# Two attention layers, a mixture layer and 64 experts on one core: a new order of pieces on every engine, and maxima rows in two transfers in place of four

## The chip, the cores and the metric

The kernel runs on one core of a Trainium2 chip. A core has a matrix engine (TensorE; PE in the profile, its weight loads PEld), a vector engine (VectorE, DVE), a scalar engine (ScalarE, ACT), GpSimd (POOL) and SyncE (SP), each with an instruction stream of its own. The streams meet only through semaphores. Transfers are issued by SP and POOL and carried out by 16 DMA engines. The metric is device time in microseconds (us) of one launch.

## The reference

The input x has 32 sequences of 256 tokens with 256 features; a context of the same shape belongs to it. Everything is float32. Cut to what matters:

```python
x = x + xattn0(layernorm(x), ctx, ctx, Wq, bq, Wk, bk, Wv, bv, Wo, bo)   # 16 heads of 16, softmax(q k^T / 4) v
x = x + mixture(layernorm(x), P_w, U1, U2, U3, W1, W2, b2)
x = x + xattn1(layernorm(x), ctx, ctx)                                  # 16 heads of 16, no projections
x = x + moe(layernorm(x), router_w, w_gate, w_up, w_down, ws_gate_up, ws_down)

# mixture: z_i = (x P_w^T) U_i^T; C_i = softmax over the 3 largest of 12
#   h = gelu(sum_e C1[:, e] * (x W1[e]^T));  y = sum_e C2[:, e] * (h W2[e]^T) + C3 b2
# moe: probs = softmax(x router_w^T), the 8 largest of 64, weights made to sum to 1;
#   each expert takes up to 128 tokens: y = (silu(g) * u) w_down;  plus a shared expert for every token
```

## The kernel before, in words

One batch is one sequence (128 tokens x 2 tiles). The 32 batches go through the four layers one behind the other, but overlapped: while PE works on the mixture of one batch, the attention of the layers around it stands between. After them 64 expert steps follow (loads of gathered rows, gate and up, down), which the change does not touch.

The work is cut into pieces, and each engine has one long string, `ORDERS[engine]`, in which each letter is one piece; the next piece of that kind is taken each time the letter comes (`pieces`). Nothing else sets the order of the work: each engine runs its string from front to back, and where a piece needs another engine it waits for that engine's semaphore, with all that stands behind it on its own engine waiting too. In the middle of the kernel (batches 5 to 29) each string repeats itself exactly from batch to batch.

A batch has two attention jobs (layer 0 and layer 1), a job has two halves of 8 heads, and a half u is made of these pieces:

- N, `spread`: SP copies the split keys and queries of the half from HBM into `kst` and `qst` (4 transfers of 192 KB, lines 529 and 532).
- O, `s1` (4 per half, L1286): PE forms the scores of two heads in the bank `first`. The next O may only write there when DVE has read the maxima off it (`nm`, L978).
- P, `max_rows`: DVE splits the maxima into a high and a low part (`nmp`, L988 and L990), PE turns them (L1294), ACT copies them (`mT`, L787), and SP puts them into `qst` as two further rows per pair of heads, by four transfers of one row (L540).
- Q, `s2` (4 per half, L1304): PE forms the scores again, less the maximum, in the bank `second`; ACT takes the exponent (`exps`, L793) before the next Q may write there.
- R, `av` (2 per half, L1320): PE multiplies with the values; ACT copies the result (`out_sb`, L800). S, `out_turn`, turns it back (L1331).

M, `mix` (24 per batch, L1386) is one expert of the mixture: 12 matmuls of 128x256 in three splits, in the two-part bank `mixp`; DVE adds the result with its weight (L1070), and M number n waits until DVE has done number n-2. Other letters that count here: F `d_turn` and v `h_turn` (turns of activations, L1212), J `d_up` (the shared expert's down product, L1443, which also writes to `first`), p `r_turn` (turn of the mixture's input; ACT copies it as `r_part_h`, L721, DVE forms the rest `r_part_l`, L888), q `r_z` (the routing scores, L1365, which read both). O and Q use 48 and 50 of the array's rows at a time, two heads beside each other; all else named here uses its full height.

The first batches and the last ones have orders of their own, since the pipeline fills and drains there. POOL scatters the rows of each batch to the experts' slots (L678, 16 per batch); its string holds the letters O too, and a scatter waits until PE has done the O that stands ahead of it there. The last 48 scatters stand behind the last O of half 127, one behind the other, and the expert steps load their rows behind the last of them.

Of the kernel before, what the change touches and what calls it, by code (L numbers as in the profile page):

```python
# [34 lines left out]
class Steps:  # L35
# [5 lines left out]
    def up(self):  # L41
# [16 lines left out]
        "LbPczNPNAgPajNPNLbPczNPNAgPajNPNLbPczNPNAgPajNPNLbPczNPNAgPjNPNLPzNPNAPPLzNNPALPzNANWWWPWWWWPWWWWWWWWWLL"
# [1521 lines left out]
```

## Time and profile before

| | before |
|---|---|
| median of 3 runs | 2767.86 us (2764.5 to 2769.37) |
| profiled execution | 2765.2 us, span 2763.4 us |
| PE busy | 2616.3 us, 95% of the span |
| PE weight loads (beside PE) | 2189.8 us, 79% |
| DVE busy | 2207.7 us, 80% |
| ACT busy | 1067.6 us, 39% |
| POOL busy | 811.1 us, 29% |
| mean granted TensorE clock | 0.984 of full |
| chain that ended last | PE 77%, DVE 12%, issue 4%, DMA 2% |

The span runs from the first to the last instruction; the 1.8 us that the execution takes beyond it lie around it. "Idle before" names the instruction that released the engine. Busy shares of PE and DVE are of pipelined instructions: two of them that overlap are counted from start to end together.

### The profile page before, as it was taken

To read this page: it belongs to the slowest core of one execution; us is meant where nothing else is said; L and a number is where in the kernel's file an instruction comes from. 1 tells how busy PE (TensorE), PEld (TensorE's weight loads), DVE (VectorE), ACT (ScalarE), POOL (GpSimd) and SP (SyncE) were. 2 spreads that over 40 slices of the span, in tenths; PEclk is the share of its full clock that TensorE was granted. 3 is DMA by queue.
4 is the path that set the end of the run, shared out by engine and by line. 5 is a ranking of instruction groups with operands and counts; after the bars stand their busy time and mean duration, and the time that the engine had idled before them with its cause. 6 is when DMAs were issued, how large, how long until landed. Compare 5 with 4: busy or idle time off the path is not lost.

```text
span 2763.4 us, 59981 instructions
## 1 busy us (share of the span) xinstructions
PE 2616.3 (95%) x22949; PEld 2189.8 (79%) x22949; DVE 2207.7 (80%) x6135; ACT 1067.6 (39%) x1622; POOL 811.1 (29%) x829
## 2 busy tenths in 40 slices
PE   3899999999999999999999999999999999985999
PEld 3778788888888888888888888888888888863776
DVE  5677888888888888888888888888888888762554
ACT  3333434444444444433444444444444344322332
POOL 1000133322323232322332232323232232226444
PEclk9999999999999999999999999999999999986999
DMA  7644444444444444443444444444344333245997
GB/s 226 174 141 107 114 127 129 124 109 115 118 118 110 117 112 97 117 118 93 107 112 99 107 117 112 109 112 113 89 106 109 93 98 83 55 87 157 230 234 169
DMA packets 322210, 336.02 MB, mean 122 GB/s; under 512 B 46676, under 2 KB 302751, under 8 KB 321412
## 3 DMA queue, kind: packets, MB, share of 16 engines
q1 hardware_dynamic: 286404, 307.37, 42.8%
q0 software_dynamic: 33792, 18.52, 4.0%
q10 hardware_dynamic: 1728, 6.29, 0.7%
q8 instruction: 182, 2.98, 0.5%
q14 instruction: 104, 0.85, 0.1%
HBM read 191.65 MB, written 221.81 MB: 150 GB/s over the span
## 4 chain that ended last, share of the span: by engine, by line
PE 77%; DVE 12%; issue 4%; DMA 2%; ACT 2%; POOL 2%; SPq 1%; POOLq 0%; ACTq 0%; DVEq 0%
PE mixp L1386 35%; PE attn_out L1320 6%; PE second L1304 5%; DVE nm L978 4%; PE first L1286 4%; DVE hid L1070 3%; PE misc L1254 3%; PE misc L1212 3%; PE mixp L1488 3%; PE misc L1422 2%; PE misc L1331 2%; PE second L1507 2%; PE misc L1461 2%; PE misc L1350 2%; PE first L1443 2%
## 5 line engine op out<-in xcount | busy, mean ns | idle before, releaser
L793 ACT ACTIVATE exps<-second 128x1024 f32<-128x1024 f32 x512 | 525.4, 1026 | 770.9 <-PE second L1304 763.6
L678 POOL DMA_INDIRECT expert_slots<-row_mem,sidx x512 | 510.4, 997 | 820.1 <-PE first L1286 579.1
L1386 PE MATMUL mixp<-w_h,r_part_h 128*128 128x256 f32 x3072 | 664.2, 297 | 2.3 <-DVE r_part_l L888 1.1
L978 DVE TENSOR_REDUCE nm<-first 128x4 f32<-128x1024 f32 x504 | 614.3, 1219 | 24.8 <-PE first L1286 24.2
L1386 PE MATMUL mixp<-w_h,r_part_l 128*128 128x256 f32 x3072 | 609.8, 280 | 0.0
L1386 PE MATMUL mixp<-w_l,r_part_h 128*128 128x256 f32 x3072 | 609.3, 279 | 0.0
L1386 PEld LDWEIGHTS mixp<-w_h,r_part_h 128*128 128x128 f32 x3072 | 467.8, 189 | 43.4 <-issue 2.1
L1386 PEld LDWEIGHTS mixp<-w_l,r_part_h 128*128 128x128 f32 x3072 | 468.8, 188 | 0.0
L1386 PEld LDWEIGHTS mixp<-w_h,r_part_l 128*128 128x128 f32 x3072 | 468.6, 188 | 0.0
L1070 DVE SCALAR_TENSOR_TENSOR x_mem<-mixp,C,x_mem 128x256 f32<-128x256 f32 x768 | 332.6, 477 | 74.5 <-PE mixp L1386 67.5
L1070 DVE SCALAR_TENSOR_TENSOR hid<-mixp,C,hid 128x256 f32<-128x256 f32 x704 | 303.6, 477 | 54.4 <-PE mixp L1386 52.9
L652 POOL TENSOR_TENSOR norm<-norm,minus_half 128x2 f32<-128x2 f32 x128 | 91.8, 717 | 694.9 <-DVE norm L917 694.9
L1320 PE MATMUL attn_out<-exps,vx 128*17 128x256 f32 x4096 | 273.8, 389 | 4.5 <-ACT exps L793 4.5
L1304 PE MATMUL second<-qst,kst 50*128 50x256 f32 x2048 | 254.5, 319 | 9.9 <-ACT exps L793 5.5
L1286 PE MATMUL first<-kst,qst 48*128 48x256 f32 x2016 | 232.1, 307 | 18.8 <-DMA qst<-q_parts 11.4
L1304 PEld LDWEIGHTS second<-qst,kst 50*128 50x128 f32 x2048 | 163.6, 189 | 84.1 <-issue 39.7
L1286 PEld LDWEIGHTS first<-kst,qst 48*128 48x128 f32 x2016 | 155.9, 188 | 53.1 <-DMA qst<-q_parts 11.7
L1320 PEld LDWEIGHTS attn_out<-exps,vx 128*17 128x17 f32 x4096 | 95.2, 98 | 101.0 <-issue 20.5
L689 POOL DMA_INDIRECT out<-x_mem,sidx x64 | 99.0, 1546 | 112.9 <-DVE sidx L1168 48.8
L725 ACT ACTIVATE nat_h<-misc,qk_cols 128x256 fp32r<-128x256 f32 x128 | 53.6, 470 | 152.3 <-PE misc L1254 147.5
L893 DVE SCALAR_TENSOR_TENSOR nat_l<-misc,qk_cols,nat_h 128x256 fp32r<-128x256 f32 x128 | 56.0, 479 | 61.1 <-ACT nat_h L725 61.1
L800 ACT COPY out_sb<-attn_out 128x512 f32<-128x512 f32 x128 | 74.5, 582 | 78.1 <-PE attn_out L1320 74.6
(236 smaller groups left out, 3593.1 us busy)
## 6 DMA issues: line engine op xcount, KB each, us to landing
kst<-k_parts SPq DMA_DIRECT2D x256, 192.0 KB, 4.1
qst<-q_parts SPq DMA_DIRECT2D x256, 192.0 KB, 4.5
q_parts<-nat_h SPq DMA_DIRECT2D x128, 256.0 KB
k_parts<-ctx_part_h SPq DMA_DIRECT2D x64, 256.0 KB, 2.5
k_parts<-nat_h SPq DMA_DIRECT2D x64, 256.0 KB, 5.6
q_parts<-nat_l SPq DMA_DIRECT2D x64, 256.0 KB
exps<-in_wgu SPq DMA_DIRECT2D x30, 384.0 KB, 4.2
expert_slots<-row_mem SPq DMA_DIRECT2D x16, 642.0 KB, 6.5
```

Source lines behind the costliest of these rows:

```text
L652: pool.e.tensor_tensor(rstd[kind][:, :], veps[kind][:, :], minus_half[:, :], ALU.pow).then_inc(p_pow[kind], 1)
L678: pool.e.indirect_dma_start(out=slots_dram, out_offset=bass.IndirectOffsetOnAxis(ap=sidx[b % 2][:, t, k:k + 1], axis=0), in_=row[b % 2][:, ...
L689: pool.e.indirect_dma_start(out=out_pad, out_offset=bass.IndirectOffsetOnAxis(ap=eid[e % NID], axis=0), in_=ey[e % NY], in_offset=None, bo ...
L793: act.e.activation(exps[:, j % NU, :, :, :].rearrange("p k t s -> p (k t s)"), second[:, :, :].rearrange("p k s -> p (k s)"), ACT.Exp, sca ...
L978: dve.e.tensor_reduce(nm[u % 2][:, :, 2 * j:2 * j + 2].rearrange("p t k -> p k t"), (mixp_mem if in_mixp(b, kind, j) else first)[:, :, :]. ...
L1070: dve.e.scalar_tensor_tensor(acc, src, c, acc, ALU.mult, ALU.add).then_inc(v_mix, 1)
L1212: m = pe.e.transpose(v[:, dt, t * P:(t + 1) * P], src[:, t, dt * P:(dt + 1) * P], ident)
L1254: m = pe.e.matmul(out, w[j][:, dt, c * P:(c + 1) * P], x[i][:, dt, :], start=(n == 0), stop=(n == 3 * DT - 1))
L1286: m = pe.e.matmul(bank[k][:, t * S:(t + 1) * S], q_st[u % 3][at, j, t * P:(t + 1) * P], k_st[u % 3][at, j, :], start=True, stop=True)
L1304: m = pe.e.matmul(bank2[k][:, s * S:(s + 1) * S], k_st[u % 3][at, j, s * P:(s + 1) * P], q_st[u % 3][at, j, :], start=True, stop=True)
L1320: m = pe.e.matmul(attn_out[r0:r0 + HD + 1, q * S:(q + 1) * S], vx[:, s, h * H // 2 + HQ * q + i, :], exps[:, (2 * q + i // 2) % NU, i % 2, ...
L1386: m = pe.e.matmul(mixp[q % 2][:, t * D:(t + 1) * D], src[i][:, dt, t * P:(t + 1) * P], wmix[n][j][:, l, dt, :], start=(k == 0), stop=(k == ...
```

## The change

It has two parts. First, the strings in `ORDERS` are replaced for all five engines. The numbers of pieces stay as they are (SP 544, POOL 1247, ACT 1388, DVE 2348, PE 2880 in the strings), and so does what each piece computes, except for the second part. The new strings do not repeat exactly in the middle: most batches share one order, and some have two or three pieces the other way round. Second, the maxima rows: the layout of `nmp` puts the high and the low part of one group of heads beside each other, so that SP can write two rows with one transfer. A half then takes two transfers in place of four, and `c_m` counts 32 per half in place of 64.

```diff
@@ ORDERS, "pe", one batch in the middle of each string
-        "vRQOSMhQOMKRPMiMOQMSQOMlOQMmQORRPMSMMIQOMLQOMpQORQOqRPMMkOQMSMOQyMMtMQOMuQOMFRPMfMOQGMQORJ"
+        "vROSMOQhMMKRPMiMOQSMOQlMQOmQORRPMSMIMQOLMOQMpQORQOqRPMkMOQSMOQtMyMMMOQuMMOQFRPMfMOQGMQORQJ"
...
@@ max_rows on SP
-                    for part in range(2):
-                        for k in range(2):
-                            r0 = (part * 2 + k) * HP
-                            sp.e.dma_start(row_block(q_st[u % 3], k, K1 + part, 1),
-                                           mT[u % 2][r0:r0 + HP, :].bitcast(F32)).then_inc(c_m[u % 2], 16)
+                    for k in range(2):
+                        sp.e.dma_start(row_block(q_st[u % 3], k, K1, 2),
+                                       mT[u % 2][2 * HP * k:2 * HP * (k + 1), :].bitcast(F32)).then_inc(c_m[u % 2], 16)
@@ max_rows on ACT
-                    act.wait_ge(c_m[u % 2], 64 * (u // 2))
+                    act.wait_ge(c_m[u % 2], 32 * (u // 2))
@@ max_rows on DVE
-                    dve.e.tensor_copy(np_[:, :, 0, :, :], v).then_inc(v_nm, 1)
+                    dve.e.tensor_copy(np_[:, :, :, 0, :], v).then_inc(v_nm, 1)
                     dve.wait_ge(v_nm, 2 * u + 1)
-                    dve.e.tensor_tensor(np_[:, :, 1, :, :], v, np_[:, :, 0, :, :].bitcast(F32),
+                    dve.e.tensor_tensor(np_[:, :, :, 1, :], v, np_[:, :, :, 0, :].bitcast(F32),
                                         ALU.subtract).then_inc(v_nm, 1)
@@ max_rows and s2 on PE
-                                           nmp[u % 2][:, t, :, :, :].rearrange("p a k n -> p (a k n)"), identr[:, :])
+                                           nmp[u % 2][:, t, :, :, :].rearrange("p k a n -> p (k a n)"), identr[:, :])
-                    pe.wait_ge(c_m[u % 2], 64 * (u // 2 + 1))
+                    pe.wait_ge(c_m[u % 2], 32 * (u // 2 + 1))
```

The second part makes two lines of code go, so lines behind it carry a number smaller by 2 in the changed kernel (PE's L1386 is L1384 there).

Three places show what moves. In each pair the first rows are of the kernel before.

**At J.** PE at the end of a batch in the middle (batch 13 to 14): `first<-wsgu,router_mem` is J, `second` is Q, `first<-kst,qst` is O, `attn_out` is R, `misc<-identr,hid` is v.

```order
L1304 MATMUL second<-qst,kst 128x256 x4
L1286 MATMUL first<-kst,qst 128x256 x4
L1320 MATMUL attn_out<-exps,vx 17x256 x8
L1443 MATMUL first<-wsgu,router_mem 128x192 x4
L1212 MATMUL misc<-identr,hid 128x128 x4
L1320 MATMUL attn_out<-exps,vx 17x256 x8
L1304 MATMUL second<-qst,kst 128x256 x4
L1286 MATMUL first<-kst,qst 128x256 x4
L1331 MATMUL misc<-identr,out_sb 128x128 x4
```

The same place of the changed kernel:

```order
L1302 MATMUL second<-qst,kst 128x256 x4
L1284 MATMUL first<-kst,qst 128x256 x4
L1318 MATMUL attn_out<-exps,vx 17x256 x8
L1302 MATMUL second<-qst,kst 128x256 x4
L1441 MATMUL first<-wsgu,router_mem 128x192 x4
L1210 MATMUL misc<-identr,hid 128x128 x4
L1318 MATMUL attn_out<-exps,vx 17x256 x8
L1284 MATMUL first<-kst,qst 128x256 x4
L1329 MATMUL misc<-identr,out_sb 128x128 x4
```

One Q has moved from behind v and R to just ahead of J, and stands in a group of its own there; O and S behind v and R stay (20 of the 25 middle batches have this, 5 keep J right behind R).

**At P of a layer-0 half, DVE.** Between the maxima of the half's last O (`nm`) and their split (`nmp`); `hid<-mixp` is the addition of an M.

```order
L1075 TENSOR_TENSOR x_mem<-x_mem,misc 128x256 x2
L978 TENSOR_REDUCE nm<-first 128x2x2
L1070 SCALAR_TENSOR_TENSOR hid<-mixp,C,hid 128x256 x2
L988 CAST nmp<-nm 128x2x8
L990 TENSOR_TENSOR nmp<-nm,nmp 128x2x8
L912 BN_STATS norm<-x_mem 128x6 x2
```

The same place of the changed kernel:

```order
L1068 SCALAR_TENSOR_TENSOR hid<-mixp,C,hid 128x256 x2
L976 TENSOR_REDUCE nm<-first 128x2x2
L986 CAST nmp<-nm 128x4x4
L988 TENSOR_TENSOR nmp<-nm,nmp 128x4x4
L1068 SCALAR_TENSOR_TENSOR hid<-mixp,C,hid 128x256 x2
L910 BN_STATS norm<-x_mem 128x6 x2
```

The addition that stood between the maxima and their split stands behind the split now. PE has moved that M as well: its `QOMFRP` has become `MOQFRP`, so the M goes ahead of the last O, and the Q stands behind that O.

**At the same P, SP.** `qst<-mT` are P's rows, `kst<-k_parts` with `qst<-q_parts` one spread (N), `ctxT` and `kept` loads of a later batch, `k_parts<-nat_h` the store of the keys.

```order
L529 DMA kst<-k_parts 48x4x256 x2
L532 DMA qst<-q_parts 48x4x256 x2
L540 DMA qst<-mT 1x4x256 x4
L529 DMA kst<-k_parts 48x4x256 x2
L532 DMA qst<-q_parts 48x4x256 x2
L496 DMA ctxT<-in_ctx 128x2x256
```

The same place of the changed kernel:

```order
L529 DMA kst<-k_parts 48x4x256 x2
L532 DMA qst<-q_parts 48x4x256 x2
L529 DMA kst<-k_parts 48x4x256 x2
L532 DMA qst<-q_parts 48x4x256 x2
L538 DMA qst<-mT 2x4x256 x2
L472 DMA k_parts<-nat_h 128x2x256 x2
```

The spread that stood behind P's rows stands ahead of them now. It is that of the half after next, and waits until PE has done the last Q of the half before P's, the Q that PE has behind its last O now.

**At p, ACT.** `exps` is Q's exponent, `r_part_h` the copy for p.

```order
L787 CAST mT<-misc 16x256
L800 COPY out_sb<-attn_out 128x512
L793 ACTIVATE exps<-second 128x1024 x3
L721 CAST r_part_h<-misc 128x512
L793 ACTIVATE exps<-second 128x1024
L800 COPY out_sb<-attn_out 128x512
```

The same place of the changed kernel:

```order
L785 CAST mT<-misc 16x256
L798 COPY out_sb<-attn_out 128x512
L791 ACTIVATE exps<-second 128x1024 x2
L719 CAST r_part_h<-misc 128x512
L791 ACTIVATE exps<-second 128x1024 x2
L785 CAST mT<-misc 16x256
```

The copy for p has one exponent less ahead of it. PE's order there, `pQORQOqR`, is the same in both.

At the end of the layers (halves 126 and 127) PE's string was `RQRSOOOOPOOOOQ` and is `RQOORSOOOOPOOQ` now: two O of half 126 stand ahead of the last R and S of half 125, and two O of half 127 ahead of P. DVE's maxima moved along; POOL's end is as it was.

## Rows read from the trace of the kernel before

**Rows 1.** Busy time by stretch: us, busy (instructions), PE clock, DMA share, GB/s.

```profile
0.00:490.00 490.00, 426.41 (x3723) 357.93 (x3724) 372.65 (x964) 184.10 (x261) 78.00 (x104) 0.99 0.53 145
...
1000.00:1500.00 500.00, 493.28 (x4595) 420.37 (x4594) 430.98 (x1183) 207.16 (x296) 145.42 (x152) 1.00 0.44 109
...
2350.00:2560.00 210.00, 158.11 (x1208) 121.63 (x1207) 118.99 (x350) 57.76 (x82) 84.65 (x88) 0.82 0.43 103
```

**Rows 2.** Executions of line 808 in 980 to 2000 us.

```profile
L808 ACT ACTIVATE hid<-hid x14: 629/630/630, 1017.0 to 1988.8; 128x512 f32<-128x512 f32 x14
```

**Rows 3.** Waits of PE in 1000 to 1500 us: total us, times, longest.

```profile
PE first L1443 <- DVE nm L978: 3.1, 7, 0.4
PE misc L1365 <- DVE r_part_l L888: 1.5, 6, 0.3
PE misc L1294 <- DVE nmp L990: 1.4, 7, 0.2
PE second L1304 <- DMA qst<-mT: 0.6, 1, 0.6
```

**Rows 4.** Timeline at line 1443: start us, us, engine, line, [idle before <-releaser].

```profile
1014.42 0.40 PE L1286 MATMUL first<-kst,qst 48*128 48x256 f32 x4
...
1014.99 1.22 DVE L978 TENSOR_REDUCE nm<-first 128x4 f32<-128x1024 f32 x1
...
1016.26 1.57 PE L1443 MATMUL first<-wsgu,router_mem 128*128 128x192 f32 x8 [0.45 <-DVE nm L978]
```

**Rows 5.** Timeline at line 1294, the transpose of the maxima.

```profile
1001.84 0.50 PE L1286 MATMUL first<-kst,qst 48*128 48x256 f32 x4
...
1003.14 1.22 DVE L978 TENSOR_REDUCE nm<-first 128x4 f32<-128x1024 f32 x1
...
1004.28 0.87 DVE L1070 SCALAR_TENSOR_TENSOR hid<-mixp,C,hid 128x256 f32<-128x256 f32 x2
...
1005.26 0.18 DVE L990 TENSOR_TENSOR nmp<-nm,nmp 128x16 fp32r<-128x16 f32 x1
...
1005.58 0.28 PE L1294 MATMUL misc<-identr,nmp 128*16 128x128 f32 x2 [0.21 <-DVE nmp L990]
```

**Rows 6.** Timeline ahead of line 1365, the routing scores.

```profile
1055.10 1.02 ACT L793 ACTIVATE exps<-second 128x1024 f32<-128x1024 f32 x1 [1.76 <-PE second L1304]
...
1055.34 1.23 DVE L978 TENSOR_REDUCE nm<-first 128x4 f32<-128x1024 f32 x1
1056.02 0.58 ACT L721 CAST r_part_h<-misc 128x512 fp32r<-128x512 f32 x1
...
1056.63 0.69 DVE L888 TENSOR_TENSOR r_part_l<-misc,r_part_h 128x512 fp32r<-128x512 f32 x1
```

**Rows 7.** Timeline from the maxima's transfers to the exponent matmul that reads them.

```profile
1006.28 2.44 SPq L540 DMA_DIRECT2D qst<-mT  x4
...
1008.77 0.93 SPq L529 DMA_DIRECT2D kst<-k_parts  x2
...
1010.43 0.40 PE L1304 MATMUL second<-qst,kst 50*128 50x256 f32 x4
```

**Rows 8.** DMA issues, from the page: count, KB each, us to landing.

```profile
qst<-q_parts SPq DMA_DIRECT2D x256, 192.0 KB, 4.5
```

**Rows 9.** Chain that ended last, 1019 to 1032 us: start us, us, what.

```profile
1019.79 0.23 PE first L1286 x4
...
1029.40 1.41 PE mixp L1386 x12
...
1031.48 1.60 PE mixp L1386 x12
```

**Rows 10.** Chain that ended last, 2475 to 2486 us.

```profile
2475.96 3.29 DVE nm L978 x3
...
2485.34 0.80 PE mixp L1286 x4
```

**Rows 11.** Timeline of POOL at the first of the last 48 scatters.

```profile
2487.03 1.06 POOL L678 DMA_INDIRECT expert_slots<-row_mem,sidx  x1 [3.58 <-PE mixp L1286]
```

More of the change, by code:

```diff
@@ L58 @@
[L58 removed]
+        "bacgVjNbaNcPgaPbjNVVNVcVPgVVjNPVNVPVaVVVVPbVzcNNgPAajNPVNbPczNPNPAagjNPLNbPczNPNgAPajNPLNbPzNNPgPAajNPLNcbPczN"
+        "NPgPAajNPLNbPczNNPgPAajNPLNbPczNNPgPAajNPLNbPczNNPgPAajNPLNbPczNNPgPAajNPLNbPczNNPgPAajNPLNbPczNNPgPAajNPLNbPc"
+        "zNNPgPAajNPLNbPczNNPgPAajNPLNbPczNNPgPAajNPLNbPczNNPgPAajNPLNbPczNNPgPAjaNPLNbPczNNPgPAajNPLNbPczNNPgPAajNPLNb"
+        "PczNNPgPAajNPLNbPczNNPgPAajNPLNbPczNNPgPAajNPLNbPczNPNgPAajNPLNbPczNNPgPAjNPLNabPczNNPgPAajNPLNbPczNNPgPAajNPL"
@@ new lines @@
+        "OOTOTOTwcCTOOTDOTdOTOOTOTTOTOTOTBOTOTTnOOTOTOTwcCTOOTDOTdOTOOTOTTOTOTOTBOTOTTnOOTOTOTwcCTOOTDOTdOTOOTOTTOTOTOT"
+        "BOTOTTnOOTOTOTwcCTOOTDOTdOTOOTOTBTOTOTOTOTOTTnOOTOTOTwcCTOOTDOTdOTOOTOTTOTOTOTBOTOTTnOOTOTOTwcCTOOTDOTdOTOOTOT"
+        "TOTOTOTBOTOTTnOOTOTOTwTcCOOTDOTdOTOOTOTTOTOTOTBOTOTTnOOTOTOTwcCTOOTDOTdOTOOTOTTOTOTOTBOTOTTnOOTOTOTwcCTOOTDOTd"
+        "OTOOTOTTOTOTOTBOTOTTnOOTOTOTcwCTOOTDOTdOTOOTOTTOTOTOTBOTOTTnOOTOTOTwcCTOOTDOTdOTOOTOTTOTOTOTBOTOTTnOOTOTOTwcCT"
+        "OOTDOTdOTOOTOTTOTOTOTBOTOTTnOOTOTOTwcCTOOTDOTdOTOOTOTTOTOTOTBOTOTTnOOTOTOTwcCTOOTDOTdOTOOTOTTOTOTOTBOTOTTnOOTO"
@@ new lines @@
+        "QtPfQQsRRvFPQGQhKQRRiQlQQPQRRQpQQPRRrckQtyQQQFPfQGQsRRvQQhKPRRiQlQQQRRPQQpQQPRRrckQtQyQQFPfQGQsRRvQhQKRRPiQQlQ"
+        "QPRRQQpQQPRRrckQtQyQQFPfQGQsRRvQQhKRRPiQQlQQPRRQQpQQPRRrckQtQyQQFPfQGQsRRvQQhKRRPiQQlQQPRRQQpQQPRRrckQtQyQFQPf"
+        "QGQsRRvQQhKRRPiQQlQQPRRQQpQQPRRrckQtQyQQFPfQGQsRRvQhQKRRPiQQlQQPRRQQpQQPRRrckQtQyQQFPfQGQsRRvQhQKRRPiQQlQQPRRQ"
+        "QpQQPRRrckQtQyQQFPfQGQsRRvQQhKRRPiQQlQQPRRQQpQQPRRrckQtQyQQFPfQGQsRRvQQhKRRPiQQlQQPRRQQpQQPRRrckQtQyQQFPfQGQsR"
+        "RvQQhKRRPiQQlQQPRRQQpQQPRRrckQtQyQQFPfQGQsRRvQQhKRRPiQlQQQPRRQQpQQPRRrckQtQyQFPfQQGQsRRvQQhKRRPiQQlQQPRRQQpQQP"
@@ new lines @@
+        "OQMpQORQOqRPMkMOQSMOQtMyMMuMOQMMOQFRPMfMOQGMQORQJvROSMOQhMMKRPMiMOQSMQOlMQOmQORRPMSMIMQOLMOQMpQORQOqRPMkMSOQMO"
+        "QtMyMMMQOuMMOQFRPMfMQOGMQORJvQROSMOQhMMKRPMiMOQSMOQlMQOmQORRPMSMIMOQLMQOMpQORQOqRPMkMSOQMQOtMyMMuMQOMMOQFRPMfO"
+        "QMGMQORQJvROSMOQhMMKRPMiMOQSMQOlMQOmQORRPMSMIQOMLMOQMpOQROQqRPOMkMQOSMtQOMyMMuQOMMQMFMMPOGMQORRJvOQMSOQMQOMKRP"
+        "MMRQMSOQMlOQQOmRRPMSMIMQLQMMpQQqRRMyMMSMMMMtMFMMOGOMMJuOvOMKMMMMPOMIMOMLMOMQOMMQRPQyQRQQSQRQOORSOOOOPOOQQFPQRQ"
+        "GJQRQQKIQSRRSLFGJIKL"
```

134 lines of the change are left out of this document (58 added, 76 removed).

## The prediction

> **What bounds the kernel now.** I read the busy time by stretch first. Between 1000 and 1500 us PE is busy for 493.28 of 500 us, while DVE has 430.98 and ACT 207.16; before 490 us PE has 426.41 of 490, and from 2350 to 2560 us 158.11 of 210, at a mean granted clock of 0.82 [rows 1]. So the middle is bound by PE's own work, with 1.3% of it idle, and the two ends by waits. The table of one line's executions gives the period: line 808 runs once per batch, and its 14 executions start at 1017.0 to 1988.8 us, so a batch takes 971.8 / 13 = 74.75 us [rows 2]. The list of waits of PE in the same 500 us (6.69 batches) names nearly all of the 6.7 us: J for DVE's maxima 3.1, q for `r_part_l` 1.5, P for `nmp` 1.4, Q for the maxima rows' transfer 0.6 [rows 3]. Per batch that is 0.46, 0.22, 0.21 and 0.09 us, 0.98 in all. This is what a new order can win in the middle, 25 batches long: 24.5 us at most, unless it also makes PE's work itself shorter.
>
> **J.** PE starts the last O ahead of J at 1014.42, DVE its reduction at 1014.99 with 1.22 us, and J starts at 1016.26, when PE has been idle for 0.45 [rows 4]. J cannot start sooner in the new order: the same O and the same reduction stand ahead. But PE has a Q to do in the idle time, one that stood behind v and R. The second of two such pieces in a row takes 0.23 us, and one that stands alone costs more, because the switch between the full array and 48 or 50 rows is paid: 12 matmuls of an M take 1.41 us behind another M and 1.60 behind a piece of another kind [rows 9], so 0.19 us at the far side of a group. The moved Q stands in a group of its own (16 groups of Q and O per batch become 17). The wait of 0.46 goes, 0.20 comes back for the group: -0.26 per batch, in the 20 batches that have it; in the 5 others nothing is won. I keep -0.46 and 0 as ends.
>
> The Trainium skill, "TensorEngine Tiling (Array Packing)", section "Tiling Modes" (Key Properties), says that changing the tiling mode drains the array. The 0.19 us of [rows 9] agree with it. The rule speaks against this change, which has more such changes per batch than before, and it leads to the first rival below.
>
> **P of the layer-0 half.** The last O starts at 1001.84; DVE starts its reduction only at 1003.14, since an addition of x stands ahead; then the addition of an M at 1004.28 with 0.87; the split ends at 1005.44 and P starts at 1005.58, after 0.21 idle [rows 5]. In the new order DVE does the M behind the split. The reduction can start when O is done, 0.40 behind its start, and started 0.57 behind it where DVE was not held longer [rows 4]; then come 1.14 (1003.14 to 1004.28), 0.09, two splits of 0.19 and 0.14 to PE: 2.15 to 2.33 us from O to P. PE's own work from O to P was 1005.58 - 1001.84 - 0.21 = 3.53 us with an M in it; without the M (1.5, between the two of [rows 9]) and with the Q (0.23) it is 2.26. So 0 to 0.07 of the wait stays, and I take -0.18. What is late next is DVE's own M, on which the second M behind P waits: it is done 0.9 us behind the split, and PE has P and an M (1.4) in between.
>
> **q.** ACT takes an exponent at 1055.10 for 1.02 us and only then the copy `r_part_h` at 1056.02; DVE's rest follows at 1056.63 with 0.69, and q waits up to 0.3 for it [rows 3, 6]. The copy now has that exponent behind it, and even if it started only when the exponent did, it would be done at 1055.68; DVE's rest is then held by the reduction alone, until 1056.56. It comes 0.1 us sooner at most, and the exponent ends later, by up to 0.58 us if the copy starts no sooner, and the next Q with it. PE's p ends about 0.5 before that exponent's start, so I expect 0.1 to 0.2 of it, beside an R of PE. I take -0.10 of the 0.22, between -0.22 and +0.2.
>
> **The maxima rows.** SP's four issues take 2.44 us, and the Q that reads them starts 4.85 us behind P (1005.58 to 1010.43) [rows 5, 7]. Two take half, so the last row lands 1.2 us sooner. PE waited for this only 0.09 us per batch; that goes: -0.09. The rest is slack. It is used up elsewhere: the spread of the half after next (at 1008.77, behind P's rows [rows 7]) now stands ahead of them. It waits for the Q that PE has just behind its last O, some 1.8 us before P, and its four issues of 0.93 per two end at about P + 0.3; P's copy on ACT is ready for SP at P + 0.7. So SP is not late. Its data, 768 KB, land 4.5 us from issue [rows 8], the last at about P - 0.6 + 4.5 = P + 3.9, and if the rows come behind them on the queue they come at about P + 4, against P + 4.85 wanted. I count it at nothing, with 0.9 us to spare, and with the second rival as the other end. DVE's copy and subtraction and PE's transpose of the maxima keep their sizes: nothing.
>
> **What comes back.** The other exchanges (an M past an O, a Q past a v) leave the number of groups. Where an M now stands right behind another, or an S right behind O, the pieces ahead have less time; from the spacing of the pieces I see two such places with 0.1 to 0.3 us to spare. I give 0.1 us per batch for them, between 0 and 0.3.
>
> Per batch: -0.26 x 20/25 = -0.21, -0.18, -0.10, -0.09, +0.10, together -0.48; times 25 it is -12.0 us. The batches before 490 us lose 63.6 us to waits [rows 1], mostly for the first loads, which the change leaves; the same four places in them and fewer groups: -1.3 (about 0.25 for each of five batches), between 0 and -4.
>
> **The end of the layers.** From 2475.96 DVE does four reductions at a stretch (3.29 for three), PE and POOL wait for them, and the last O starts at 2485.34 [rows 10]. Two of the eight reductions are taken under the exponents of the half before now: 2 x 1.13 = 2.3 us sooner. Nothing behind is reached otherwise: POOL's first scatter starts at 2487.03, released by that O [rows 11], 47 more follow it in a row, and the expert steps behind them. The whole tail shifts: -2.3, between 0 (if the clock, 0.82 there, falls lower) and -3.7.
>
> The sum is -12.0 - 1.3 - 2.3 = -15.6 us. The profiled execution took 2765.2 us (a span of 2763.4 and 1.8 around it), which gives 2749.6; the median of the runs, 2767.86, is 2.7 above it, so 2752.3.
>
> **Rivals.**
> First, no change. The idle time only moves: each wait of [rows 3] ends where another engine's instruction ends, and with DVE busy for 86% of the middle [rows 1] each reduction moved delays another. And the array's switches cost more than 0.2: an M behind a group is 0.19 longer at its far side, and the near side costs up to the same, 0.4 per group. Then J brings 0.06, DVE gives back 0.3 to 0.4, and the middle is at -0.1 x 25 = -2.5; with the end's -2.3 it is 2763. For it: many small pieces exchanged for small gains. Against it: the four waits are named, and three of the four go without a new group.
>
> Second, slower. The maxima rows queue behind the spread. If the spread's wait for Q ends 1 us later than I think, its four issues hold SP until P + 1.3, its last data land at P - 0.6 + 1 + 4.5 = P + 4.9, the rows, issued until P + 2.5, land a little behind them, at up to P + 5.8, and Q, with everything of PE behind it, waits 1.0 us at one of four P per batch: +25 us, less the 15.6 of the rest: 2765.2 + 9.4 + 2.7 = 2777. It decides from the point where the rows land later than P + 4.85. For it: 768 KB are ahead of 8 rows, on one queue, and one wait of 0.6 us for the rows' transfer is already in the list [rows 3]. Against it: SP's issues are spread over the batch, the transfers' share is 0.44 in the middle [rows 1], and two transfers fewer make 1.2 us of room.
>
> Third, more than forecast. The groups cost nothing in sum, and all 0.98 us go: -24.5, and with -5 at the ends it is 2738.
>
> **How the numbers follow.** The forecast with its own range of 2743 to 2761 has a chance of 0.62, the first rival 0.18, the second 0.10, and the third 0.10. What a measurement can tell from no change is about 0.2%, 5.5 us: faster means below 2762.3. The first rival at 2763 lies at this border, and I give a third of it to faster: 0.62 + 0.10 + 0.06 = 0.78, less 0.03 for a forecast that is half lost: 0.75. Slower is 0.10 (the second rival, with some smaller loss of its kind), the same 0.15. The range goes from 2739 (just above the third rival) to 2766, past the first; it leaves out the second rival and about half of the third.
>
> **What would show it.** In the profile of the changed kernel: the period of the gelu line at 74.75 - 0.48 = 74.3 us; PE waits for `nm` at J near 0 where a Q stands ahead; for `nmp` at the layer-0 half's P near 0; for `r_part_l` about half; SP's issue of the rows with 1.2 us; no wait of Q for `qst<-mT` above 0.1 us per batch (the second rival shows some 0.5 to 1 there); idle PE in 1000 to 1500 us near 3 instead of 6.7; the sum of PE's matmul time higher by about 0.2 per batch (the first rival: 0.4 and more, and new waits for DVE); and the first scatter 2.3 us nearer to the last S of the layers. The forecast is wrong if the period moves by less than 0.1 us, or if the first or last stretch moves by over 5 us.

## The result

| | before | changed |
|---|---|---|
| median of 4 runs each | 2766.18 us (2763.79 to 2769.37) | 2816.32 us (2811.27 to 2822.89) |
| ratio | 1 | 1.0182, 95% interval 1.0158 to 1.0206 |
| span of the profiled execution | 2763.4 us | 2809.5 us |
| PE busy | 2616.3 us | 2649.1 us |
| DVE busy | 2207.7 us | 2245.5 us |

The forecast was 2752.3 us with a range of 2739 to 2766; the change makes the kernel 50 us slower. The profile after, in the views of [rows 1 to 3]: first the busy time of the middle stretch.

```profile
1000.00:1500.00 500.00, 492.99 (x4512) 415.93 (x4510) 434.93 (x1171) 203.88 (x292) 144.77 (x151) 1.00 0.43 106
```

The gelu line, all executions between 980 and 2000 us:

```profile
L806 ACT ACTIVATE hid<-hid x13: 630/630/631, 1029.6 to 1945.6; 128x512 f32<-128x512 f32 x13
```

The waits of PE between 1000 and 1500 us:

```profile
PE mixp L1384 <- DVE hid L1068: 1.7, 7, 0.3
PE second L1302 <- DMA qst<-mT: 1.1, 4, 0.4
PE misc L1292 <- DVE nmp L988: 1.1, 6, 0.2
PE misc L1210 <- DVE xhat L937: 0.7, 1, 0.7
PE first L1441 <- DVE nm L976: 0.4, 1, 0.4
PE first L1284 <- DVE nm L976: 0.2, 1, 0.2
```

The period is (1945.6 - 1029.6) / 12 = 76.33 us in place of 74.75 [rows 2]. Two waits of [rows 3] are gone or nearly so: J for `nm` 3.1 to 0.4, q for `r_part_l` 1.5 to nothing. P's wait for `nmp` (1.4 to 1.1) has mostly moved: it was 0.20 us per batch at the layer-0 half's P and is 0.08 there now, but 0.18 at the last half's P, where it was nothing. And still PE does 83 fewer matmul records in the 500 us while it is "busy" as long as before. A PE that is paced by others shows as busy here, since its matmuls overlap and their ends are modelled. The list of waits can't say where 1.6 us per batch went. The starts of the pieces can. The table has the mean time in us between P (L1292) and G (the logits, L1420) in batches 8 to 26. P1 is the layer-0 half's P of [rows 5], P3 the P two halves later; a row starts and ends at the M behind the P that comes once more between P3 and the next P1:

| stretch | before | changed | C late | C and spread late | three back | two rows and J |
|---|---|---|---|---|---|---|
| to P1 | 20.77 | 21.78 | 20.93 | 20.93 | 20.93 | 20.67 |
| P1 to G | 5.17 | 5.73 | 5.80 | 5.17 | 5.17 | 5.18 |
| G to P3 | 31.99 | 31.80 | 31.78 | 31.77 | 31.54 | 31.73 |
| P3 to the next batch | 16.69 | 16.89 | 16.93 | 17.00 | 17.21 | 16.70 |
| sum | 74.62 | 76.20 | 75.44 | 74.87 | 74.85 | 74.28 |

(The columns behind "changed" are experiments below: a_pool_late_again, a_pool_sp_late, a_three_back and b2_J.) So 1.01 of the 1.58 us lie ahead of P1, 0.56 between P1 and G, 0.20 behind P3, and 0.19 are won between. The 24 periods from the 6th gelu to the 30th have 38.8 us of the 46.1 by which the span grew (76.38 us each in place of 74.76).

A mean hides that the batches are not alike. Over these 24 periods "C late" has 75.81 us, and not 75.44: it has four long ones (77.3 to 78.8 us), and two of these lie behind the batches of the table.

**Ahead of P1.** The timeline of DVE and POOL in the changed kernel, batch 15:

```profile
1231.99 0.42 DVE L999 TENSOR_TENSOR ctx_o<-misc,rsum 128x256 f32<-128x256 f32 x1
...
1232.33 1.70 DVE L937 TENSOR_SCALAR xhat<-x_mem,norm 128x256 f32<-128x256 f32 x2
...
1232.49 1.39 POOL L664 TENSOR_TENSOR x_mem<-x_mem,ctx_o 128x512 f32<-128x512 f32 x1 [0.55 <-DVE ctx_o L999]
...
1233.96 0.86 DVE L1068 SCALAR_TENSOR_TENSOR hid<-mixp,C,hid 128x256 f32<-128x256 f32 x2
...
1234.28 0.60 PE L1210 MATMUL misc<-identr,xhat 128*128 128x128 f32 x4
...
1236.79 0.39 PE L1384 MATMUL mixp<-w_h,r_part_h 128*128 128x256 f32 x1 [0.24 <-DVE hid L1068]
```

And the same instruction in the kernel before:

```profile
1214.46 0.74 DVE L939 TENSOR_SCALAR xhat<-x_mem,norm 128x256 f32<-128x256 f32 x2
```

The two halves of `xhat` take 1.70 us in place of 0.74, and they end (1234.03) just after POOL's addition, which ran from 1232.49 to 1233.88. The first half started before POOL did and took 0.4; the second took 1.38. In the changed kernel both are released by the same thing, the `ctx_o` of S: DVE's next piece is x, and POOL's next is C, the addition into `x_mem`. Over the whole kernel, DVE's groups of this kind, changed kernel (columns: busy us, mean ns, idle before):

```profile
L937 DVE TENSOR_SCALAR xhat<-x_mem,norm 128x256 f32<-128x256 f32 x192 | 101.8, 572 | 1.4 <-POOL norm L650 1.4
...
L986 DVE CAST nmp<-nm 128x16 fp32r<-128x16 f32 x128 | 31.5, 246 | 2.0
```

and before:

```profile
L939 DVE TENSOR_SCALAR xhat<-x_mem,norm 128x256 f32<-128x256 f32 x192 | 72.3, 418 | 5.6 <-POOL norm L652 4.2
...
L988 DVE CAST nmp<-nm 128x16 fp32r<-128x16 f32 x128 | 21.9, 171 | 2.0
```

By instruction: 27 of the long `xhat` overlap POOL's L664 (27.4 us beyond the median in sum), 25 a scatter (4.5 us), and 27 of the `nmp` copies a scatter (7.5 us). Before there were 3.3 us of all such excess. DVE's other large groups kept their length (L1068: 476 ns in both).

The Trainium skill, "SBUF — State Buffer", section "Who interferes with whom", says that DVE in a mode that uses two ports and GpSimd take one shared pair of ports in turn, each for a whole instruction, and that the later one waits until the other has ended. The trace agrees: 1.38 us of a 0.41 us instruction, ended 0.15 us behind POOL's, and the same 0.14 to 0.16 us in all 27 meetings. That a port is what the two share is the page's reading; the trace shows that one waits for the other. The prediction did not weigh this rule.

**Between P1 and G.** SP and PE of the changed kernel around the P at 1017.77:

```profile
1016.21 0.79 SPq L529 DMA_DIRECT2D kst<-k_parts  x2
1017.04 0.93 SPq L532 DMA_DIRECT2D qst<-q_parts  x2
1018.48 1.29 SPq L538 DMA_DIRECT2D qst<-mT  x2
```

```profile
1015.43 0.50 PE L1284 MATMUL first<-kst,qst 48*128 48x256 f32 x4
...
1017.77 0.29 PE L1292 MATMUL misc<-identr,nmp 128*16 128x128 f32 x2
...
1022.99 0.50 PE L1302 MATMUL second<-qst,kst 50*128 50x256 f32 x4 [0.19 <-DMA qst<-mT]
```

P itself came as forecast, 2.34 us behind O and without a wait. SP was not late either (rows issued at P + 0.71, two in 1.29 us). But the rows landed 3.2 us behind the end of their issue; in [rows 7] the Q that reads them started 1.7 us behind it. The spread's 768 KB are ahead of them.

Over the whole kernel PE waits for these rows 20 times, 10.4 us in sum, and three of the waits are of 1.2 to 1.7 us, more than the second rival's 1.0. The longest costs more than itself:

```profile
1554.88 0.70 PE L1302 MATMUL second<-qst,kst 50*128 50x256 f32 x4 [1.66 <-DMA qst<-mT]
1555.50 0.80 PE L1384 MATMUL mixp<-w_h,r_part_h 128*128 128x256 f32 x2
1556.10 0.63 PE L1384 MATMUL mixp<-w_h,r_part_l 128*128 128x256 f32 x2
```

```profile
1555.00:1558.40 3.40, 3.40 (x17) 3.18 (x18) 0.70 (x1) 1.02 (x1) 0.00 (x0) 0.50 0.69 229
```

Right behind it the granted clock is 0.50 (1.2 in place of 2.4 GHz) for 3.4 us, and two matmuls take 0.63 us in place of 0.40. In this batch P1 to G is 8.6 us; the median of the batches is 5.65. The same wait in after_again, 1.7 us, had no such fall behind it. In the kernel before the clock does not fall between 490 and 2340 us.

**J**, in the changed kernel:

```profile
1104.70 1.22 DVE L976 TENSOR_REDUCE nm<-first 128x4 f32<-128x1024 f32 x1
...
1105.46 0.50 PE L1302 MATMUL second<-qst,kst 50*128 50x256 f32 x4
1105.97 1.57 PE L1441 MATMUL first<-wsgu,router_mem 128*128 128x192 f32 x8
```

J starts 0.05 us behind the reduction's end, as in [rows 4], with a Q done in what was idle time.

### The profile page after: what moved, and what is told of

The parts are those of the page before. It is cut to its first block, busy times and chain, and to the rows that moved or that the text cites. A ratio compares the mean times of both kernels' runs of the same rounds, so it can differ in the third digit from the quotient of the medians.

```text
span 2809.5 us, 59707 instructions
## 1 busy us (share of the span) xinstructions
PE 2649.1 (94%) x22949; PEld 2200.0 (78%) x22949; DVE 2245.5 (80%) x6135; ACT 1066.4 (38%) x1622; POOL 809.3 (29%) x829
## 4 chain that ended last, share of the span: by engine, by line
PE 62%; DVE 22%; DMA 6%; issue 5%; POOL 2%; ACT 2%; SPq 2%; DVEq 0%; POOLq 0%; ACTq 0%
PE mixp L1384 26%; DVE nm L976 7%; PE first L1284 4%; PE attn_out L1318 4%; PE second L1302 4%; PE mixp L1486 3%; DMA qst<-mT 3%; PE misc L1210 3%; DVE hid L1068 3%; PE misc L1252 2%; PE misc L1420 2%; PE second L1505 2%; DVE xhat L937 2%; PE misc L1459 2%; PE misc L1329 2%
## 5 line engine op out<-in xcount | busy, mean ns | idle before, releaser
L1384 PE MATMUL mixp<-w_h,r_part_h 128*128 128x256 f32 x3072 | 668.5, 299 | 13.5 <-DVE hid L1068 6.2
L1384 PE MATMUL mixp<-w_h,r_part_l 128*128 128x256 f32 x3072 | 612.2, 281 | 0.0
L1384 PE MATMUL mixp<-w_l,r_part_h 128*128 128x256 f32 x3072 | 610.7, 280 | 0.0
L1384 PEld LDWEIGHTS mixp<-w_h,r_part_h 128*128 128x128 f32 x3072 | 472.3, 190 | 53.1 <-DVE hid L1068 18.4
L1384 PEld LDWEIGHTS mixp<-w_l,r_part_h 128*128 128x128 f32 x3072 | 471.3, 189 | 0.0
L1384 PEld LDWEIGHTS mixp<-w_h,r_part_l 128*128 128x128 f32 x3072 | 471.0, 189 | 0.0
L1068 DVE SCALAR_TENSOR_TENSOR x_mem<-mixp,C,x_mem 128x256 f32<-128x256 f32 x768 | 327.1, 476 | 32.2 <-PE mixp L1384 31.4
L1068 DVE SCALAR_TENSOR_TENSOR hid<-mixp,C,hid 128x256 f32<-128x256 f32 x704 | 305.4, 475 | 28.6 <-PE mixp L1384 25.7
L1302 PE MATMUL second<-qst,kst 50*128 50x256 f32 x2048 | 240.1, 312 | 22.2 <-ACT exps L791 10.5
L1284 PE MATMUL first<-kst,qst 48*128 48x256 f32 x2016 | 238.2, 313 | 21.8 <-DMA qst<-q_parts 13.4
L937 DVE TENSOR_SCALAR xhat<-x_mem,norm 128x256 f32<-128x256 f32 x192 | 101.8, 572 | 1.4 <-POOL norm L650 1.4
```

The source lines that it names most:

```text
L937: dve.e.tensor_scalar(dst[:, t, 0:D], src[:, t, :], mv[kind][:, t, 0:1], rstd[kind][:, t:t + 1], ALU.subtract, ALU.mult).then_inc(v_norm[k ...
L1068: dve.e.scalar_tensor_tensor(acc, src, c, acc, ALU.mult, ALU.add).then_inc(v_mix, 1)
L1284: m = pe.e.matmul(bank[k][:, t * S:(t + 1) * S], q_st[u % 3][at, j, t * P:(t + 1) * P], k_st[u % 3][at, j, :], start=True, stop=True)
L1302: m = pe.e.matmul(bank2[k][:, s * S:(s + 1) * S], k_st[u % 3][at, j, s * P:(s + 1) * P], q_st[u % 3][at, j, :], start=True, stop=True)
L1384: m = pe.e.matmul(mixp[q % 2][:, t * D:(t + 1) * D], src[i][:, dt, t * P:(t + 1) * P], wmix[n][j][:, l, dt, :], start=(k == 0), stop=(k == ...
```

## Experiments

Two theories on the 50 us: A, DVE's `xhat` and POOL's addition meet on a shared port; B, `xhat` is merely late in DVE's order. A third is the forecast's second rival, the rows behind the spread. The first four kernels ran on a chip on which the kernel before takes 2782.27 us; only ratios are compared.

**POOL's piece back (a_pool_late).** POOL's string, per batch:

```diff
-wcCTOOT
+wcTOOTC
```

> The changed kernel with one piece moved on POOL alone: in 26 batches the addition into x_mem (L664, letter C) goes behind the next scatter, where the kernel before had it; DVE's and PE's strings stay. Theory A, a shared port: DVE's scaling xhat<-x_mem,norm (L937) is held for as long as POOL's addition beside it runs (1.38 us in place of 0.41). Then its mean falls from 572 ns to about 420, DVE is 27 us less busy, the waits of M and y at that place (about 0.8 us per batch) go, and the time falls by 15 to 25 us, to about 2796. Theory B, order alone: xhat is late since a reduction and S stand ahead of it in DVE's string; POOL has no part in it, xhat's length is due to something else, and the time stays at 2816 within 3 us.

Measured: 1.0182 (1.0165 to 1.0198). Neither theory had that as it was written: the meeting was gone (`xhat` held for 12.2 us in sum in place of 31.9) and so was the wait at y, and yet nothing was won. PE had a new wait, which hides the gain (a_pool_late_again below is without it):

```profile
PE misc L1329 <- ACT out_sb L798: 25.6, 28, 1.9
```

**DVE's piece back (a_x_early).** DVE's string:

```diff
-rMwMOSxMOMy
+rMwMxOSMOMy
```

> The changed kernel with one piece moved on DVE alone: in 28 batches xhat of the layer-1 norm (letter x) goes ahead of the reduction and S, where the kernel before had it. Theory A: xhat then runs before POOL's addition and is 0.41 us again; 15 to 25 us are won, as by moving POOL's piece. Theory B: xhat comes 1.9 us sooner, all of the wait of y goes; 15 to 25 us are won here, but not by moving POOL's piece. A third theory, that the loss lies in the maxima rows queued behind the spread: nothing is won by either, since about 10 us lie there and 36 elsewhere unexplained.

Measured: 1.0333 (1.0317 to 1.0350), much slower, which no theory foresaw. The new wait is here too (24.8 us), PE waits for `nm` at O for 45.6 us in place of 7.9, and ten times in the middle the granted clock falls to 0.5 for 3.4 us. And `xhat` has only changed partners: 24 of them now meet POOL's `ctx_part_l` (L645), 22.9 us beyond the median.

```profile
L937 DVE TENSOR_SCALAR xhat<-x_mem,norm 128x256 f32<-128x256 f32 x192 | 97.8, 550 | 2.7 <-POOL norm L650 1.3
```

That it grows beside another addition of POOL, at another place, and again ends 0.15 us behind it, speaks for A. The time of this run says little on either theory, since the new wait and the clock are in it. It also shows that a piece's old place in one engine's string is not its old place in time.

**The transfers alone (b_two_rows).** The kernel before with the diff's second part, orders as before.

> The kernel before with the second part of the change alone: two transfers of two rows, the orders as before. If the transfers are harmless, as I forecast, the waits of Q for the rows (3.6 us in all) go and SP's issue of them falls from 2.3 to 1.2 us; the time is 0 to 4 us below before. Rival: two rows per transfer, or the new layout of nmp on DVE and PE, cost something themselves, and part of the 50 us comes back here.

Measured: 0.9985 (0.9976 to 0.9994), -4.5 us. The transfers were as good as forecast (2.3 us) or better, and no part of the loss.

**Both moves in the kernel before (b_both_moved).**

```diff
@@ pool
-wTcOOTC
+wTcCOOT
@@ dve
-rMwMxOSMMOy
+rMwMOSxMMOy
```

> The kernel before (old orders, four transfers) with only the two pieces moved as in the changed kernel: POOL's addition C early, DVE's xhat behind the reduction and S, in 25 batches each. Theory A: the meeting of the two is made here, xhat grows to a mean of about 560 ns, and PE waits about 0.8 to 1.3 us per batch at y: +20 to +33 us. Theory B: y waits for the 1.9 us by which xhat is later, less what PE has in between: 0 to +15 us, with xhat at 418 ns.

Measured: 1.0143 (1.0127 to 1.0158), +41 us: two pieces moved in 25 batches make most of the loss. `xhat` has 583 ns, and PE waits for it:

```profile
L939 DVE TENSOR_SCALAR xhat<-x_mem,norm 128x256 f32<-128x256 f32 x192 | 104.0, 583 | 6.4 <-POOL norm L652 6.3
```

```profile
PE misc L1212 <- DVE xhat L939: 22.2, 26, 1.8
```

**DVE's move alone (b_x_late)**, the kernel before with only the second of these edits, separates order from port.

> The kernel before with one move on DVE alone: xhat of the layer-1 norm (x) behind the reduction and S, in 25 batches; POOL's addition C stays late, so the two don't meet there. With both moved the ratio was 1.0143. Theory A (port): xhat stays 0.41 us, y waits little or nothing, ratio 1.000 to 1.005. Theory B (order): the ratio is near 1.014 without POOL's part.

Measured: 1.0036 (1.0023 to 1.0049), as A had it. The order alone costs 10 us; the same order beside POOL's addition costs 41 (by ratio, on the two chips). Of the 1.16 us per batch between the two kernels, 1.13 lie in the stretch to P1. POOL's piece alone in the kernel before was not tried, so this pair doesn't exclude that it costs something without the meeting; PE's waits for `xhat`, 22.2 us, are most of the 31 between the two. The mean is 442 ns, since 23 of the `xhat` touch `ctx_part_l` for a moment (5.9 us in sum):

```profile
L939 DVE TENSOR_SCALAR xhat<-x_mem,norm 128x256 f32<-128x256 f32 x192 | 77.1, 442 | 4.3 <-POOL norm L652 4.2
```

**The changed kernel again (after_again)**, as a base on a chip like the first (before: 2766.91 us).

> The changed kernel as it is, beside the others of this call on one chip, since the first four runs were on a chip on which the kernel before takes 2782 us in place of 2766. If chips don't matter, the ratio is 1.018 again. In the two kernels made from the changed one on that chip, but not in the changed kernel's own profile, PE waits 1.0 us per batch at an S for out_sb, 25 times. If the chip does it, this run has that wait too and a ratio of about 1.027; if POOL's or DVE's moved piece did it, this run has no such wait.

Measured: 1.0159 (1.0144 to 1.0175), no wait for `out_sb`.

**POOL's piece alone, on such a chip (a_pool_late_again).**

> The changed kernel with POOL's addition C moved alone, as in a_pool_late, which ran on the chip where the kernel before takes 2782 us and where PE waited 1.0 us per batch for out_sb at one S. If that wait belongs to that chip, it is absent here: the ratio is 1.016 less 0.75 to 0.86 us x 26, so about 1.008 to 1.009, and moving the spread as well (1.0031) was worth 0.45 us x 25, 0.4%. If the wait belongs to the moved piece, the ratio is about 1.018 again.

Measured: 1.0086 (1.0070 to 1.0101), the number of A. The stretch to P1 falls by 0.85 us, from 21.78 to 20.93, and `xhat` to 469 ns:

```profile
L937 DVE TENSOR_SCALAR xhat<-x_mem,norm 128x256 f32<-128x256 f32 x192 | 82.2, 469 | 1.4 <-POOL norm L650 1.4
```

**The spread behind P's rows as well (a_pool_sp_late)**: SP's `zNNPg` is `zNPNg` again.

> The changed kernel with POOL's addition C behind the scatter and the second spread of each layer-0 pair behind P's rows again (25 batches), as both stood before. If the rows behind the spread are what Q waits for (0.3 to 0.6 us in about half of the layer-0 halves, 8 to 10 us in all), those waits go, and this is 8 to 10 us faster than the same with POOL's piece alone (ratio 1.018): about 1.014 to 1.015. If the rows' own way through ACT and SP is what is late, nothing changes.

Measured: 1.0031 (1.0019 to 1.0043). Against POOL's piece alone on a like chip (1.0086) it wins 0.55%, 15 us; I had expected 8 to 10. From P1 to G it is 5.17 us, as before; 5.80 with the spread ahead. The rival's mechanism is there, at 0.6 us per batch. The long batches and the three falls of the clock in the middle of a_pool_late_again are gone with it, and over the 24 periods it is 0.76 us per batch (75.81 to 75.05).

**A third meeting undone (a_three_back).** POOL's `OTTn` at the last half is `nOTT` again.

> The changed kernel with three things as before: POOL's addition C, the spread on SP, and POOL's power of the norm (nR, L650) ahead of the half's last O again, which delays the scatter that now runs while DVE copies the maxima of half 3 of 4 (L986: 0.46 us in place of 0.17, 25 times). Theory A: that copy is short again, P there comes 0.2 to 0.3 us sooner per batch, and the ratio falls from 1.0031 to about 1.001. If the copy's length comes from something else, 1.003 stays.

Measured: 1.0039 (1.0026 to 1.0052). The copy is short again,

```profile
L986 DVE CAST nmp<-nm 128x16 fp32r<-128x16 f32 x128 | 24.1, 188 | 2.0
```

and P3 comes 0.23 us sooner (G to P3 31.54). The mean of the stretch behind it is 0.21 larger, but that is one batch of 19, with 21.6 us there where the others have a mean of 17.0. In it Q waited for the rows, and then the granted clock was 0.50 for 6.8 us:

```profile
1574.75 0.50 PE L1302 MATMUL second<-qst,kst 50*128 50x256 f32 x4 [1.51 <-DMA qst<-mT]
```

```profile
1575.60:1582.40 6.80, 6.80 (x28) 5.86 (x28) 2.50 (x4) 0.72 (x1) 0.00 (x0) 0.50 0.23 71
```

The other batches keep the 0.2 us, so the expectation on the copy held there; in the profiled execution this one batch, 4.6 us too long, takes back nearly all of it. Whether the other executions had such a batch is not known. What is left over the kernel before is for the most part no wait that the profile names: between 1000 and 1500 us the waits add up to 1.2 us, and the longest is

```profile
PE first L1441 <- DVE nm L976: 0.4, 1, 0.4
```

The mean batch still takes 74.85 us against 74.28 with the order of before and J moved.

**J alone (b2_J)**, with the two transfers:

```diff
-QORJvRQOS
+QORQJvROS
```

> The kernel before with two transfers of rows and one move on PE in 26 batches: a Q from behind v and R to just ahead of J. The forecast's term: the wait of 0.46 goes and 0.2 comes back for one more group of Q and O, -0.26 per batch, so 6 to 7 us faster than two transfers alone (ratio 0.9985), about 0.996. Rival: a group of its own costs more than 0.2 us, up to 0.45, and there is no gain.

Measured: 0.9959 (0.9945 to 0.9972). The gelu line starts at 1014.8 to 1982.1 in 13 periods, 74.41 us each; 74.58 with the transfers alone:

```profile
L806 ACT ACTIVATE hid<-hid x14: 629/630/630, 1014.8 to 1982.1; 128x512 f32<-128x512 f32 x14
```

```profile
L806 ACT ACTIVATE hid<-hid x14: 629/630/630, 1014.9 to 1984.5; 128x512 f32<-128x512 f32 x14
```

That is 0.18 us per batch, 4.6 us, for the term of 0.26; the ratios (0.9985 on one chip, 0.9959 on another) put it at 7 us.

**P alone (b2_P)**, with the two transfers:

```diff
@@ pe
-MuQOMFRP
+MuMOQFRP
@@ dve
-OMP
+OPM
```

> The kernel before with two transfers of rows and the exchange at P of the layer-0 half alone, in 27 batches: on PE the M ahead of O, Q behind O, on DVE the M's addition behind the split of the maxima. The forecast's term: -0.18 per batch, 4 to 5 us faster than two transfers alone, ratio about 0.997. Theory A adds: the split's copy (L986) now comes while POOL's scatter, released by the same O, runs, and is held by 0.1 to 0.3 us; then the gain is 0 to 2 us.

Measured: 0.9989 (0.9980 to 0.9998), nothing beyond the transfers (0.9985). The wait of P for `nmp` is gone from PE's list between 1000 and 1500 us, which has only J's for `nm` and q's for `r_part_l`. But from u (the bias product of the mixture, `misc<-b_rows,mT`) to P it is 4.38 us, where it was 4.30. The copy of the maxima did not meet the scatter here (excess 0.2 us in all), so A's addition to the expectation was wrong for this place. What ate the gain is PE. u uses 36 rows of the array and stood in one group with Q and O (b_two_rows):

```profile
999.22 0.39 PE L1402 MATMUL misc<-b_rows,mT 36*128 36x256 f32 x1
999.22 0.50 PE L1302 MATMUL second<-qst,kst 50*128 50x256 f32 x2
...
999.78 0.51 PE L1284 MATMUL first<-kst,qst 48*128 48x256 f32 x4
1000.22 0.51 PE L1384 MATMUL mixp<-w_h,r_part_h 128*128 128x256 f32 x2
```

Now it stands alone, with an M on either side (b2_P):

```profile
998.94 0.51 PE L1402 MATMUL misc<-b_rows,mT 36*128 36x256 f32 x2
999.38 0.50 PE L1384 MATMUL mixp<-w_h,r_part_h 128*128 128x256 f32 x2
...
1000.98 0.51 PE L1284 MATMUL first<-kst,qst 48*128 48x256 f32 x4
1001.32 0.40 PE L1302 MATMUL second<-qst,kst 50*128 50x256 f32 x4
1001.65 0.66 PE L1210 MATMUL misc<-identr,row_mem 128*128 128x128 f32 x4
```

From start to start, u, Q and O together took 1.00 us and take 0.44 + 0.67 = 1.11 now; the M takes 1.60 in place of 1.51, and F 0.59 in place of 0.53. One more group has cost about 0.27 us, and the wait that went was 0.2.

**The version made of what worked (b2_J_q_tail)**: the two transfers, J, ACT's `QQQpQ` as `QQpQQ` in 28 batches, and at the end PE's `RQRSOOOOPOOOOQ` as `RQOORSOOOOPOOQ` with DVE's to match.

> The kernel before with two transfers of rows, the Q ahead of J, ACT's copy for p ahead of one exponent (28 batches), and the changed kernel's order of the last two halves on PE and DVE. Forecast's terms: J gave 7 us (0.9959 with the transfers); q -0.10 x 28 = -2.8 us; the end of the layers -2.3 us. Sum: a ratio of about 0.994. Rival: the exponent that now comes later delays the next Q by as much as q wins, and the end's order wins nothing: 0.996.

Measured: 2749.78 us, 0.9937 (0.9923 to 0.9951), faster than both kernels, by the sum that was expected. The batch takes 74.13 us in place of 74.28 (the q term: -0.15), and the last matmul of the last O starts 55.3 us behind the last gelu where it was 58.1 (-2.8). From the last gelu to the end of the span it is 333.7 us in place of 335.5.

## Why the prediction was wrong

Two terms that the sum put at little or nothing made the loss, and both lie in what the new order puts beside other work: "What comes back" (+0.10 us per batch; DVE's x beside POOL's C alone took 0.85), and the spread ahead of P's rows ("at nothing", measured 0.6). A third, the number of groups, took back the gain at P.

**J: right.** Forecast -0.26 per batch, measured -0.18 by period and up to -0.27 by ratio.

**P of the layer-0 half: right on the wait, wrong on the sum.** The wait went and the chain took 2.34 us, but the 0.18 us came back (b2_P). The step that failed is "The other exchanges (an M past an O, a Q past a v) leave the number of groups." The count was of groups of Q and O; u uses 36 rows and belongs to such a group too, and in the new order it stands between full-array pieces. With u counted, the PE string has 16 groups in every middle batch of the kernel before and 18 in 18 of the 25 of the changed kernel, where the prediction has 17. The price of one was 0.27 us in b2_P, not far from the 0.20 of the prediction; the count was wrong, not the price. The batch that the diff shows is no typical one in this: its u stands in a group. In PE's changed string, in fact, no two of the 25 batches are in the same order.

**q: right.** -0.10 forecast, -0.15 measured.

**The maxima rows: right on the transfers, wrong on the spread.** The two transfers gave 4.5 us (1.7 to 6.7; forecast 2.3). The spread ahead of them was counted "at nothing, with 0.9 us to spare". SP's times were right (P + 0.7). The rows' landing was not: Q started at P + 5.2, 0.4 to 0.6 us after it could have. It was the second rival, with a chance of 0.10, but at 0.6 us in the mean batch and not 1.0, with a few of 1.2 us and more; and it decided from the point named there. What neither the sum nor the rival had is the clock, which fell to 0.5 behind some of these waits (once in the middle of the changed kernel, three times in a_pool_late_again).

**What comes back: the step that failed.** The sum had +0.10 per batch "between 0 and 0.3" for pieces with less time than before. DVE's x behind O and S was one of them, and it cost 0.85 us with POOL's C beside it (a_pool_late_again), 0.85 of the 1.58 us per batch. That rests on a mistake of kind: I took each instruction's duration from the trace of before as its own, and they hold only while POOL's additions and scatters fall elsewhere. In the trace of before they nearly always did, with 3.3 us of excess in 2763. But two of its `xhat` took 1.35 and 1.44 us beside POOL's `ctx_part_l`, and the page of the Trainium skill cited above states the rule, so the warning was there. And POOL's string was changed as well, C ahead of two scatters and two O, and I did not set POOL's and DVE's pieces beside each other.

**The start and the end.** At the end -2.3 was forecast. The last O is 2.8 us nearer to the last gelu in b2_J_q_tail, and 1.0 and 2.5 in the two profiles of the changed kernel. But from the last gelu to the end of the span it is 335.8 us before, 333.7 in b2_J_q_tail, and 337.0 and 336.2 in the changed kernel: there nothing of it arrived, and why wasn't tried. At the start -1.3 was forecast, and the 6th gelu came 2.2 us later (493.5 to 495.7). These are single profiles, and the experiments made from the kernel before have 491.9 to 497.9 there, so 2 us at the start say nothing.

The sum over the changed kernel, by ratios on like chips: 1.0159, of which POOL's C takes 0.73% (20 us), the spread's place 0.55% (15 us), and what remains 0.31%. (By the periods of single profiles it is 0.57 us per batch for C and 0.76 for the spread, so which is the larger is open.) The two transfers, J, q and the end would have given -0.63%. So about 0.9%, 26 us, lie elsewhere. The profiles of a_three_back and b2_J_q_tail, 24.7 us apart in span, say where. One batch with the slow clock has 4.6 of it. The stretches before the 6th gelu and behind the 30th have 7.0. The other 23 periods have 13.1, and in them a_three_back has 18 groups more (443 against 425 in the middle batches), by 0.20 to 0.27 us each some 4 to 5 us. M also takes a mean of 1.538 us from its start to the next piece's in a_three_back, against 1.504 in b2_J, 24 times per batch; the slow clock and short waits of M are in this mean. What makes up the rest, about 8 us in the middle and the 7 around it, was not shown.

## What to carry to other kernels

Before moving pieces in several engines' orders, write down which instructions of DVE and GpSimd will run at the same moment: here a scaling on DVE beside an addition on GpSimd took as long as that addition. Count the groups with every piece that uses part of the array, not only with those that move. A duration from a trace is that of its neighbourhood. Read the single batches as well as the mean: one in 19 made a gain look like none. And take a change of orders apart: the two transfers, the Q ahead of J, p's copy and the end's order, taken alone, would have won 17 us.

## What the runs showed of the hardware

- A 0.41 us scaling of 128x256 on DVE took 1.38 us beside a 1.39 us addition on GpSimd; beside a scatter it took 0.18 us more, and a 0.17 us copy of 128x16 up to 0.47. The means of DVE's SCALAR_TENSOR_TENSOR and of its reductions from PSUM were 0.48 and 1.22 us in both kernels.
- Behind a wait of PE of 1.66 us the granted clock fell to 0.5 for 3.4 us (changed kernel), behind one of 1.51 us for 6.8 us (a_three_back). Behind one of 1.7 us in after_again it did not fall.
- Two transfers of 8 KB, issued 0.5 us behind four of 192 KB on the same queue, landed 3.2 us behind the end of their issue. Without these ahead, in [rows 7], the Q that reads the rows started 1.7 us behind it.
- On the chip where the kernel before takes 2782 us, in both kernels made from the changed one, and in no kernel elsewhere, the transposes of the last half's P reached ACT 1.2 us late, 25 times in one kernel. The profile has PE's instruction at its usual time and ACT's copy late (DVE, PE and ACT of a_pool_late):

```profile
1290.83 0.18 DVE L988 TENSOR_TENSOR nmp<-nm,nmp 128x16 fp32r<-128x16 f32 x1
...
1291.16 0.28 PE L1292 MATMUL misc<-identr,nmp 128*16 128x128 f32 x2 [0.18 <-issue]
...
1292.64 0.36 ACT L785 CAST mT<-misc 16x256 fp32r<-16x256 f32 x1 [2.77 <-PE misc L1292]
```

The same kernel elsewhere had 0.04 us there, and a ratio of 1.0086 in place of 1.0182. Whether the chip or the moment did it was not tried.
